# Gated delta rule: decay rows broadcast by DMA, tail decay moved to the keys one chunk ahead

## The reference

```python
def step(state, xs):
    q_t, k_t, v_t, g_t, b_t = xs
    state = state * jnp.exp(g_t)[..., None, None]
    kv = jnp.einsum('bhk,bhkv->bhv', k_t, state)
    delta = (v_t - kv) * b_t[..., None]
    state = state + jnp.einsum('bhk,bhv->bhkv', k_t, delta)
    out = jnp.einsum('bhk,bhkv->bhv', q_t, state)
    return (state, out)
...
_, outs = jax.lax.scan(step, state0, xs)
```

## Time and profile before

| | us |
|---|---|
| median of 3 runs (1463.66 to 1470.07) | 1465.13 |
| span of the profiled execution | 1464.3 |
| PE busy | 1315.5 |
| DVE busy | 963.0 |
| ACT busy | 792.5 |
| POOL busy | 752.4 |

### The profile page before, as it was taken

The page is one execution under the profiler, slowest core; times in us unless marked ns, Lnnn a source line. Parts: engine busy times, 40 slices in busy tenths (PEclk is TensorE's granted clock), DMA queues, the critical chain, the costliest instruction groups (busy, mean ns, idle before and its releaser), DMA issues. The chain is left out here.

```text
span 1464.3 us, 24950 instructions
## 1 busy us (share of the span) xinstructions
PE 1315.5 (90%) x8680; PEld 880.2 (60%) x8680; DVE 963.0 (66%) x1922; ACT 792.5 (54%) x1947; POOL 752.4 (51%) x1245
## 2 busy tenths in 40 slices
PE   5768999999999999999999999988898899599994
PEld 3356666666666666666666666665545466455673
DVE  5857777778787787877878778665603466531454
ACT  4546766676666766767667576664422455310121
POOL 1775775856858568586685766841000000125363
PEclk9879999999999999999999999999998999789997
DMA  3434356364463544545445445355003930033487
GB/s 88 126 63 113 71 146 148 84 161 100 131 149 92 164 89 130 145 101 156 112 115 137 112 145 117 94 154 169 22 0 118 335 101 1 2 116 107 100 187 189
DMA packets 233180, 171.71 MB, mean 117 GB/s; under 512 B 163746, under 2 KB 202998, under 8 KB 230240
## 3 DMA queue, kind: packets, MB, share of 16 engines
q1 hardware_dynamic: 226912, 161.59, 40.7%
q0 software_dynamic: 6144, 8.53, 3.3%
HBM read 104.64 MB, written 65.83 MB: 116 GB/s over the span
## 5 line engine op out<-in xcount | busy, mean ns | idle before, releaser
L1267 DVE SCALAR_TENSOR_TENSOR heads_y<-psum_banks,gdn_conv_w,heads_y 128x1021 f32<-128x1021 f32 (+2 forms) x192 | 244.7, 1275 | 9.3 <-ACT heads_y L1072 4.8
L776 PE MATMUL psum_banks<-main_hT,gdn_w_in 128*128 128x512 f32 x512 | 242.5, 608 | 6.2 <-DMA gdn_w_in<-in_w_in 4.0
L1562 POOL TENSOR_TENSOR heads_XT<-heads_XT,heads_tmp 128x126 f32<-128x126 f32 (+22 forms) x496 | 207.8, 419 | 38.9
L1559 POOL TENSOR_TENSOR heads_tmp<-heads_XT,heads_A 128x126 f32<-128x126 f32 (+22 forms) x496 | 180.0, 363 | 39.9
L776 PEld LDWEIGHTS psum_banks<-main_hT,gdn_w_in 128*128 128x128 f32 x512 | 97.1, 195 | 95.5 <-issue 91.4
L1530 POOL TENSOR_TENSOR heads_og<-heads_og,heads_fac 128x512 f32<-128x512 f32 x60 | 60.5, 1041 | 137.5 <-DVE heads_fac L1333 137.5
L890 PE MATMUL psum_banks<-heads_w_z,main_hT 128*128 128x256 f32 x512 | 121.8, 381 | 0.0
L1095 ACT ACTIVATE heads_O<-psum_banks,heads_coef 128x128 f32<-128x128 f32 x224 | 70.0, 364 | 95.6 <-PE psum_banks L807 95.2
L1072 ACT ACTIVATE heads_y<-psum_banks,gdn_conv_w 128x1024 f32<-128x1024 f32 x64 | 71.5, 1117 | 91.7 <-PE psum_banks L776 91.7
L1288 DVE SCALAR_TENSOR_TENSOR heads_S<-heads_S,heads_coef,psum_banks 128x128 f32<-128x128 f32 x192 | 57.3, 340 | 86.9 <-PE psum_banks L830 86.4
L1278 DVE SCALAR_TENSOR_TENSOR heads_X<-psum_banks,heads_coef,heads_v_s 128x128 f32<-128x128 f32 x224 | 67.9, 345 | 65.2 <-PE psum_banks L805 65.2
(11 more groups left out here) (295 smaller groups left out, 3010.2 us busy)
## 6 DMA issues: line engine op xcount, KB each, us to landing
values_by_tokens<-heads_v_s SPq DMA_DIRECT2D x64, 256.0 KB, 4.3
heads_v_s<-values_by_tokens SPq DMA_DIRECT2D x16, 1024.0 KB, 5.5
outputs_by_features<-heads_ogT SPq DMA_DIRECT2D x120, 128.0 KB, 2.6
heads_ogT<-outputs_by_features SPq DMA_DIRECT2D x30, 512.0 KB, 3.8
main_w_gu<-in_w_gu SPq DMA_DIRECT2D x4, 2816.0 KB, 20.7
gdn_w_in<-in_w_in SPq DMA_DIRECT2D x16, 512.0 KB, 5.1
heads_A<-kk_blocks SPq DMA_DIRECT2D x64, 128.0 KB, 4.8
keys_by_tokens<-heads_k_tok SPq DMA_DIRECT2D x64, 128.0 KB, 3.3
```

Of the source, the lines that this page charges most:

```text
L776: ins = pe.matmul(out[:, half * 512:(half + 1) * 512], w_in[:, kd_, j * P:(j + 1) * P], hT[:, kd_, half * 512:(half + 1) * 512], start=kd_ ...
L1267: dve.scalar_tensor_tensor(y[j][:, shift:T], src[:, 0:T - shift], conv_w[:, head, j, t:t + 1], y[j][:, shift:T], ALU.mult, ALU.add).then_i ...
L1559: pool.tensor_tensor(tmp[:, 0:n, 0:m], bc_last(XT[:, 0:n, j], m), bc_mid(A0[:, j, j + 1:BLK], n), ALU.mult).then_inc(solve_step.sem, 1)
L1562: pool.tensor_tensor(XT[:, 0:n, j + 1:BLK], XT[:, 0:n, j + 1:BLK], tmp[:, 0:n, 0:m], ALU.add).then_inc(solve_step.sem, 1)
```

## The change

**Decay.** The small tiles `row_from` and `row_to` and the 16 products of PE go, and so does the wait of these products for their banks. SP's work `gates` stands first in SP_PLAN, in every step but the first for the same step's pair: as soon as the inverse of the pair before is done (the last reader of `Dm`), it broadcasts the pair's 16 rows of cum, 8 KB, to all 128 partitions of `Dm` (1 MB). DVE adds `limit` to it in place, in the plan rows in which it took the minimum before. The term -cum of the other index is now a per-partition bias of the exponential; it differs per tile, so ACT makes sixteen exponentials of 128 columns where there were four of 512.

**Tail.** ACT writes no `Dt`. Behind `Dl` of chunk c it scales the keys of chunk c+1 by TAIL into one of two buffers `k_tail` (two instructions of 128 x 128, reading SBUF); those of chunk 0 are made ahead of `Dl` of chunk 0. `su` becomes two products of 128 columns, one per value head, with `k_tail` as weights and `Dl` moving.

The places in PE_PLAN, ACT_PLAN and DVE_PLAN stay as they are, but for the decay products, which are gone. The diff also cuts the gate and output projections into functions that can run in pieces; no plan uses pieces.

```diff
-6: decay0/3 decay1/2 decay2/0 decay3/1
+6:
...
-SP_PLAN = """kt_out inverse_out kt_in inverse_in values_out products_out values_in products_in gates
+SP_PLAN = """gates kt_out inverse_out kt_in inverse_in values_out products_out values_in products_in
 outputs_out0 outputs_in0 outputs_out1 outputs_in1 w_z w_in w_o""".split()
...
+    if name == "gates":
+        return h in INVERT and h > 0
...
             def gate_rows(h):
-                for sign, rows in enumerate([row_to, row_from]):
-                    src = cum_rows[sign, IT * h:IT * (h + 1)].rearrange("(g s) t -> g s t", g=4)
-                    sp.dma_start(rows[h % 2][sign:P:32], src).then_inc(s_rows[h % 2], 16)
+                src = cum_rows[IT * h:IT * (h + 1)].rearrange("(o s) t -> o (s t)", o=1)
+                sp.dma_start(flat(Dm[:]), src.to_broadcast([P, IT * P])).then_inc(rows_in.sem, 16)
...
                 elif name == "gates":
-                    b = bank_of(h, "decay3")
-                    sp.wait_ge(full[b].sem, full[b].done(h, "decay3"))
-                    gate_rows(h + 2)
+                    sp.wait_ge(uf_ready.sem, uf_ready.end(h - 1))
+                    gate_rows(h)
...
                     if c < C - 1:
-                        if c == 0:
-                            pe.wait_ge(kt_loaded.sem, kt_loaded.end(h - 1) * 16)
-                        pe.wait_ge(dt_ready.sem, dt_ready.done(h, f"dt{c}"))
-                        pe.matmul(flat(bank_a[:, 0:2]), k_tok[old][:, c], flat(Dt[:]), start=True, stop=True).then_inc(a_full.sem, 1)
+                        pe.wait_ge(tail_ready.sem, tail_ready.done(h, f"kt{c}"))
+                        for e in range(HD):
+                            ins = pe.matmul(bank_a[:, e], k_tail[c % 2][:, e], Dl[:, e], start=True, stop=True)
+                        ins.then_inc(a_full.sem, 1)
...
-                elif name == "decay0":
-                    for s in range(4):
-                        for g in range(4):
-                            r, out = slice(32 * g, 32 * g + 2), bank[bank_of(h, f"decay{g}")]
-                            ins = pe.matmul(out[:, s], row_from[par][r, s], row_to[par][r, s], start=True, stop=True)
-                            if s == 3:
-                                ins.then_inc(full[bank_of(h, f"decay{g}")].sem, 1)
...
+            def tail_keys(h, c):
+                if c > 1:
+                    act.wait_ge(a_full.sem, a_full.done(h, f"su{c - 2}"))
+                elif h > 1:
+                    act.wait_ge(a_full.sem, a_full.base(h))
+                for e in range(HD):
+                    i = c * HD + e
+                    ins = act.activation(k_tail[c % 2][:, e], k_tok[(h - 1) % 2][:, c], ACT.Copy, scale=coef[:, TAIL, h - 1, i:i + 1])
+                ins.then_inc(tail_ready.sem, 1)
...
                 elif part == 1:
+                    if c == 0:
+                        act.wait_ge(kt_loaded.sem, kt_loaded.end(h - 1) * 16)
+                        tail_keys(h, 0)
                     act.wait_ge(a_full.sem, a_full.done(h, f"tx{c}"))
                     act.activation(flat(Dl[:]), flat(bank_a[:, 0:2]), ACT.Copy).then_inc(dl_ready.sem, 1)
-                    if c < C - 1:
-                        for e in range(HD):
-                            i = c * HD + e
-                            ins = act.activation(Dt[:, e], bank_a[:, e], ACT.Copy, scale=coef[:, TAIL, h - 1, i:i + 1])
-                        ins.then_inc(dt_ready.sem, 1)
+                    if c + 1 < C - 1:
+                        tail_keys(h, c + 1)
...
                 if name.startswith("exp"):
-                    b = bank_of(h, f"decay{u}")
-                    act.wait_ge(free[b].sem, free[b].done(h, f"decay{u}"))
-                    part = flat(Dm[:, 4 * u:4 * u + 4])
-                    act.activation(part, part, ACT.Exp).then_inc(dm_ready.sem, 1)
+                    act.wait_ge(dm_masked.sem, dm_masked.done(h, str(u)))
+                    for it in range(4 * u, 4 * u + 4):
+                        ins = act.activation(Dm[:, it], Dm[:, it], ACT.Exp, bias=coef[:, NCUM, h, it:it + 1])
+                    ins.then_inc(dm_ready.sem, 1)
...
+                if name.startswith("decay"):
+                    dve.wait_ge(rows_in.sem, rows_in.end(h) * 16)
+                    part = Dm[:, 4 * u:4 * u + 4]
+                    dve.tensor_tensor(part, part, bc_mid(limit[:], 4), ALU.add).then_inc(dm_masked.sem, 1)
+                    return
...
-                elif name.startswith("decay"):
-                    dve.wait_ge(full[b].sem, full[b].done(h, name))
-                    dve.tensor_tensor(Dm[:, 4 * u:4 * u + 4], bank[b][:], bc_mid(limit[:], 4), ALU.min).then_inc(free[b].sem, 1)
```

More of the change, by code:

```diff
@@ L151 @@
 G_, NGAM, GAM, TAIL, GAMC, BETA = range(6)
+NCUM = G_
 NQ = 6
@@ L353, in plan, with unit @@
     return {0: PE_FIRST, 1: PE_SECOND, HK + 1: PE_LAST}.get(h, PE_PLAN)
+def unit(name):
+    return name.partition(".")[0]
 def bank_of(h, name):
-    return next(b for row in plan(h) for n, b in row if n == name)
+    return next(b for row in plan(h) for n, b in row if unit(n) == name)
 def bank_plan(h, bank):
-    return [name for row in plan(h) for name, b in row if b == bank and belongs(h, name)]
+    return list(dict.fromkeys(unit(name) for row in plan(h) for name, b in row if b == bank and belongs(h, name)))
 def pe_row(h, k):
@@ L451, in heads @@
     z = a.sb("z", [P, C, HD * P])
-    row_from = [a.sb(f"row_from{i}", [P, 4, P]) for i in range(2)]
-    row_to = [a.sb(f"row_to{i}", [P, 4, P]) for i in range(2)]
     limit = a.sb("limit", [P, P])
@@ L478, in heads @@
     Dl = a.sb("Dl", [P, HD, P])
-    Dt = a.sb("Dt", [P, HD, P])
+    k_tail = [a.sb(f"k_tail{i}", [P, HD, P]) for i in range(2)]
     og = [a.sb(f"og{i}", [P, IT, P]) for i in range(2)]
@@ L546, in heads @@
     dl_ready = per_head("delta_ready", *[f"dl{c}" for c in range(C)], steps=SCAN)
-    dt_ready = per_head("dt_ready", *[f"dt{c}" for c in range(C - 1)], steps=SCAN)
+    tail_ready = per_head("tail_keys_ready", *[f"kt{c}" for c in range(C - 1)], steps=SCAN)
     o_summed = per_head("outputs_summed", *[f"o{c}" for c in range(1, C)], steps=SCAN)
@@ L561, in heads @@
     q_root_ready = per_head("query_root_ready", "it")
-    s_rows = [a.sem(f"gate_rows{i}_loaded") for i in range(2)]
-    s_ones, s_limit = a.sem("rows_of_ones"), a.sem("limit_written")
+    rows_in = per_head("gate_rows_loaded", "it")
+    s_limit = a.sem("limit_written")
+    dm_masked = per_head("decay_rows_masked", "0", "1", "2", "3")
     dm_ready = per_head("decay_masked", "0", "1", "2", "3")
@@ L651, in _ @@
                     sp.dma_start(beta_rows[p0:p0 + 32], by_block[e]).then_inc(s_bload, 16)
-            sp.wait_ge(s_ct, 2)
-            for sign in range(2):
-                sp.dma_start(cum_rows[sign].rearrange("(half p) t -> p half t", p=P), cum_t[:, sign]).then_inc(s_cstore, 16)
+            sp.wait_ge(s_ct, 1)
+            sp.dma_start(cum_rows.rearrange("(half p) t -> p half t", p=P), cum_t).then_inc(s_cstore, 16)
             sp.wait_ge(pair_full.sem, 4)
@@ L772, in _, with project @@
         def _(pe):
-            def project(u, out):
+            def project(u, out, piece=None):
                 j, half = u // 2, u % 2
-                for kd_ in range(KD):
+                for kd_ in range(KD) if piece is None else [piece]:
                     ins = pe.matmul(out[:, half * 512:(half + 1) * 512], w_in[:, kd_, j * P:(j + 1) * P],
                                     hT[:, kd_, half * 512:(half + 1) * 512], start=kd_ == 0, stop=kd_ == KD - 1)
-                if half:
+                if half and piece != 0:
                     ins.then_inc(pair_full.sem, 1)
@@ L852, in product @@
                     pe.wait_ge(act_ready.sem, act_ready.done(h, "sq"))
-                elif name == "decay0":
-                    pe.wait_ge(s_rows[par], 32 * (h // 2 + 1))
-                    for g in range(1, 4):
-                        more = free[bank_of(h, f"decay{g}")]
-                        wait(pe, more, more.ahead(h, f"decay{g}"))
                 elif name.startswith("flip"):
@@ L908, in product @@
                 elif name.startswith("out") and h <= HK:
-                    f = slice(P * (u % 2), P * (u % 2) + P)
-                    for e in range(HD):
-                        ins = pe.matmul(flat(bank[b][:]), w_o[:, e, f], ogT[:, u // 2].rearrange("p q (c e) j -> p e c q j", e=HD)[:, e],
-                                        start=e == 0, stop=e == HD - 1)
-                    ins.then_inc(full[b].sem, 1)
+                    output_part(b, u, 0)
+                    if piece is None:
+                        output_part(b, u, 1).then_inc(full[b].sem, 1)
                 elif name.startswith("out"):
@@ L1570, in _ @@
             pool.memset(Xh[:], 0.0).then_inc(s_const, 1)
-            for i in range(2):
-                pool.memset(row_from[i][:], 1.0).then_inc(s_ones, 1)
-                pool.memset(row_to[i][:], 1.0).then_inc(s_ones, 1)
```

63 lines of the change are left out of this document (37 added, 26 removed).

## The result

The changed kernel takes 1504.26 us (median of four runs, 1498.93 to 1505.50) against 1464.99 for the kernel before: a ratio of 1.026, 95% interval 1.0229 to 1.0291. The forecast was 1482, with 1493 as the upper end. The loss is 39 us where 17 was forecast.

The account below looks back on a forecast made before the run. PE's fixed-order stream plus its stops bounds a step, with ACT the bound before chunk 3's delta copy. Steps 2 to 14 +9.6, step 1 +0.8, step 0 +1.0, clock +5.2: +16.6 on 1465.13 gives 1482 us, range 1465 to 1493.

Parts of the forecast that it names:

- The stream of a step: PE's order around chunks 3 and 4 of a head-loop step: later delta copies delay `o` of chunk 4, +0.69 us per step.
- The price of a piece: One 128-column exponential on ACT: 0.40 us long, 0.30 apart, so +0.67 us per quarter of 512 columns.
- Part 3: Tail decay moved to the keys, off the way from deltas to `su`: no gain, `su` +0.05 us per step.
- Part 5: Granted clock falling to 0.50 behind PE's longer stop: five more falls at 1.03 us, +5.2 us (0 to +11.3).
- Part 4: DVE masks and the 1 MB broadcast: no cost in steps 1 to 15, +1.0 us in step 0 through POOL's solve.
- the lock: DVE instructions with two SBUF inputs hold up POOL: a solve instruction took 1.29 us beside one, the next 0.41 alone.
- The broadcast: Rival: it takes over 14.6 us to land, delaying masks and S of chunk 2; 1522 us at 20.5; chance 0.04.
- neutral: Rival: ACT's exponential pieces start 0.24 to 0.26 us apart and the clock falls no oftener; 1465 to 1469 us; chance 0.20.
- faster case: Rival: sixteen pieces cost no more than four quarters, PE's saving of 0.57 us per step remains; 1457 us; chance 0.10.

## Why the prediction was wrong, step by step

**The stream of a step held but for one copy.** By the forecast's working `o` of chunk 3 starts 27.49 us into the step (607.46 - 579.97); it starts at 380.20 - 352.71 = 27.49. `ks` of chunk 4 was put at 29.72 and is at 29.65; `tx` at 31.15, and it is at 31.15. The stop was to be about 2.6 and is 2.52, ended by the delta copy; S is late by PE now, not by DVE; 0.27 was taken up there. Behind this, the working made ACT's copy of chunk 4 late as well. It is not: the copy ends 33.23 us into the step (385.56 + 0.38 - 352.71), 0.20 before the forecast's time, and `o` of chunk 4 follows p4 without idle time at 386.10, so its delay is the +0.50 of `tx`, not +0.69. With 0.10 more behind that point, of which 0.05 had been put down for the longer `su`, a step is 0.60 longer where 0.74 was forecast.

**The price of a piece held.** The pieces were put at 0.40 and 0.30 apart; they are 0.388, and 0.30 apart ((1.28 - 0.39) / 3). By the Trainium skill (VectorE: DVE Perf Modes, section on the errata of SBUF-source ops) a piece costs 224 cycles and one per column, 0.293 us, an estimate from its table; the trace agrees, 0.30 from start to start. Its 0.61 for a quarter is longer than the 0.54 that the kernel before showed between starts, which is why its sum came out lower.

**Part 3 held.** The tail part alone is 0.9999 of the kernel before.

**Part 5 is the step that failed, by its price.** It took 8 falls from step 1 to step 14 in place of 3, each at 1.03 us. The profiled execution has falls in eight of these steps; that the count came out is luck, as eight was picked between bounds and no row stood for it. The price was read from one step of the kernel before, with a stretch of 3.41 us behind a stop of 1.24, and taken over for a stop twice as long. Behind 2.5 us the stretches are 6.83 or 10.24, and a fall costs 2.6 to 4.3 us: +21.5 in steps 2 to 14 alone, where +5.2 stood for all. The text said that no row shows what the longer stop does, and yet let only the count of the falls move between bounds (3 to 14), not the price of one. At 4.3 us each the upper bound of eleven more falls would have been 47 us, not 11.3. The stop alone is enough for such stretches (five in the kernel before with late copies); with p4 in the stop the steps at full clock are as long and the kernel is 23.5 us faster.

**Part 4 was wrong in one step.** "POOL is through with its solve before the masks" holds in the steps from 2 on. In step 1, which starts with the solve further behind, the masks stand beside it, and the forecast had +0.8 for that step (without its fall) where +5.3 came, part of it low clock. The row used for the lock, 1.29 against 0.41, was the right one; step 1 was not looked up, where the solve of the kernel before lasts until 118.01 and its minimum instructions start at 115.82.

**The rivals.** The broadcast was not late: 5.4 us to land, where 5.5 had been read from a load of the same size. The neutral and the faster case asked for cheaper pieces, which they were not.

## What to carry to other kernels

When work is added ahead of a wait of PE, price the clock as well as the wait: look up what PE does right behind the stop, and if small products follow, don't take the price of a fall from a shorter stop. Where an instruction is split, its place decides before its cost: with the same sixteen pieces a kernel was 39 us slower than the one before when they stood ahead of a copy that PE awaits, and 4 us when the engine's idle time took them. And where a loop's first steps have other overlaps than the rest, check each added operation in those steps by itself.

## What the runs showed of the hardware that was not expected

The granted clock stayed at 1.2 GHz for 3.41 us behind a stop of 2.5 us when wide products followed (four stretches in one kernel), and for 6.83 to 10.24 us around the same stop when the small ones did (seven and nine in two kernels). A stop of 0.95 us right in front of the small products was enough for ten falls in thirteen steps, while one of 1.23 us ahead of `o` and `su` gave none in one kernel and two in each of two others, one of these 6.83 us long. Four additions of DVE with both inputs in SBUF slowed POOL's instructions from 0.24 to 0.30 us to 0.57 to 0.74; four of DVE's with one input in PSUM, beside the same instructions, did not. A broadcast of one row of 8 KB to 128 partitions landed as fast as a plain load of 1 MB, 5.4 us against 5.5 in the kernel before and 5.8 in this one.
